# A per-token attention block on one core: block-diagonal stationary filled by DMA, token index innermost

## What is computed

```python
x = x + attn(layernorm(x))
x = x + ffn(layernorm(x))
# attn: q, k, v = h @ w.T + b, each (rows, 32 heads, 32)
#   scores = einsum('bshd,bstd->bsht', q, k) / sqrt(32); probs = softmax(scores)
#   context = einsum('bsht,bstd->bshd', probs, v)
# ffn: h @ base_w.T + base_b + 2 * (LoRA of the two best of 8 experts, rank 16, softmax weights)
```

## Time and profile before

| | before |
|---|---|
| median of 3 runs | 1545.02 us |
| profiled execution: span | 1543.5 us |
| TensorE busy | 1367.9 us (89%) |
| VectorE busy | 1261.1 us (82%) |
| ScalarE busy | 503.8 us (33%) |
| GpSimd busy | 210.7 us (14%) |
| 6144 small matmuls (L956 to L958) | 983.2 us busy, 176 ns each |
| 96 copies on ScalarE, 160 on VectorE (L308) | 182.1 us and 109.9 us |
| mean granted clock | 0.986 |

### The profile page before, as it was taken

How to read it: one execution, slowest core, us unless ns; L and a number is a source line. 1 busy time by engine, 2 the same in 40 slices (tenths; PEclk the granted TensorE clock), 3 DMA queues, 4 the chain that set the end, 5 groups by cost and what they waited for, 6 DMA issues and landing times.

```text
span 1543.5 us, 30006 instructions
## 1 busy us (share of the span) xinstructions
PE 1367.9 (89%) x12432; PEld 750.4 (49%) x12432; DVE 1261.1 (82%) x1751; ACT 503.8 (33%) x572; POOL 210.7 (14%) x280
## 2 busy tenths in 40 slices
PE   0777999999999999999999999999999999999996
PEld 0444445545544554554455455445545544554553
DVE  5778888888888888888888888888888888888874
ACT  7952222333222233322223332222333222233320
POOL 0011110011111001111100111110011111001110
PEclk9989999999999999999999999999999999999997
DMA  9401111000111100011110101111000111100000
GB/s 380 165 1 42 41 41 37 31 29 25 41 41 41 37 31 29 25 41 41 41 35 33 31 23 41 41 41 36 32 31 24 41 41 41 38 30 30 24 29 28
DMA packets 20208, 70.52 MB, mean 46 GB/s; under 512 B 2144, under 2 KB 3168, under 8 KB 20192
## 3 DMA queue, kind: packets, MB, share of 16 engines
q1 hardware_dynamic: 20192, 70.30, 12.8%
HBM read 53.51 MB, written 16.78 MB: 46 GB/s over the span
## 4 chain that ended last, share of the span: by engine, by line
DVE 61%; PE 14%; issue 10%; ACT 6%; DVEq 5%; DMA 3%; SPq 0%; POOL 0%; ACTq 0%; POOLq 0%
DVE work L308 6%; DVE work L800 6%; DVE x_lo L684 5%; PE acc L965 5%; DVE work L725 5%; PE acc L976 5%; DVE work L872 4%; DVE work L843 4%; DVE work L718 4%; DMA work<-x_dram 3%; DVE work L794 3%; DVE work L889 3%; DVE work L911 3%; DVEq L751 3%; DVE work L906 2%
## 5 line engine op out<-in xcount | busy, mean ns | idle before, releaser
L1018 PE MATMUL acc<-base_parts,x_hi 128*128 128x512 f16 x1024 | 325.0, 381 | 32.4 <-DVE work L308 32.4
L956 PE MATMUL attn_ps<-work 128*128 128x32 f16 x2048 | 329.0, 177 | 2.7 <-DVE work L718 1.7
L957 PE MATMUL attn_ps<-work 128*128 128x32 f16 x2048 | 327.3, 176 | 0.0
L958 PE MATMUL attn_ps<-work 128*128 128x32 f16 x2048 | 326.9, 176 | 0.0
L957 PEld LDWEIGHTS attn_ps<-work 128*128 128x128 f16 x2048 | 189.7, 96 | 201.6
L308 ACT COPY work<-work 32x2048 f16<-32x2048 f16 x96 | 182.1, 1897 | 139.2 <-DVE work L718 88.3
L956 PEld LDWEIGHTS attn_ps<-work 128*128 128x128 f16 x2048 | 193.7, 96 | 6.0 <-issue 3.6
L965 PE MATMUL acc<-w_hi_k,x_hi 128*128 128x512 f16 x512 | 140.6, 385 | 62.1 <-DVE work L718 28.4
L1018 PE MATMUL acc<-base_parts,x_lo 128*128 128x512 f16 x512 | 194.4, 380 | 0.0
L958 PEld LDWEIGHTS attn_ps<-work 128*128 128x128 f16 x2048 | 188.9, 96 | 0.0
L668 DVE BATCH_NORM_STATS2 stats<-work 128x6 f32<-128x512 f32 x128 | 82.3, 685 | 126.4 <-DMA work<-x_dram 125.3
(11 more groups left out here) (135 smaller groups left out, 2231.4 us busy)
## 6 DMA issues: line engine op xcount, KB each, us to landing
work<-x_dram SPq DMA_DIRECT2D x64, 512.0 KB, 3.5
out_dram<-work SPq DMA_DIRECT2D x32, 512.0 KB, 2.8
work<-wT_dram SPq DMA_DIRECT2D x19, 512.0 KB, 9.5
v_parts<-wT_dram SPq DMA_DIRECT2D x8, 512.0 KB, 14.8
base_parts<-wT_dram SPq DMA_DIRECT2D x5, 512.0 KB, 12.1
biases_sb<-bias_dram SPq DMA_DIRECT2D x4, 512.0 KB, 15.2
work<-agT_dram SPq DMA_DIRECT2D x1, 544.0 KB, 4.7
lora_up<-lora_b_dram SPq DMA_DIRECT2D x1, 512.0 KB, 15.8
```

The costliest lines, as they stand in the source:

```text
L956: nc.tensor.matmul(dst, diag[:, i, 0, :], moving[:, i, 0, :], start=True, stop=False)
L957: nc.tensor.matmul(dst, diag[:, i, 0, :], moving[:, i, 1, :], start=False, stop=False)
L958: return nc.tensor.matmul(dst, diag[:, i, 1, :], moving[:, i, 0, :], start=False, stop=True)
L1018: nc.tensor.matmul(dst, rows_part[:, m // 3, :], w_part[:, m // 3, cols], start=(m == 0), stop=False)
```

## The change

The layouts of `diag`, `k_parts` and `parts` are turned: part a outermost, the token index t innermost. The transposes of q, k and v then write `turned` densely, and TensorE reads its stationary operand, and the moving operand of the scores, with a step of 32 values (64 bytes). The probabilities keep their order within a part (`probs`, another view of the same buffer), so that their moving operand stays dense. The blocks of `diag` are filled by DMA: eight copies SBUF to SBUF for q and eight for v, each of 32 partitions x 1024 fp16 (64 KB), issued by SyncE, four when the high part is there and four when the low part is. `qdiag_ready` and `vdiag_ready` count their landings. VectorE's transpose of v no longer waits for the q block (only for q's low part). The copies on ScalarE and VectorE are gone.

```diff
-        diag = carve(block_diag_len).bitcast(F16).rearrange("p (t a c) -> p t a c", t=QD, a=2)
+        diag = carve(block_diag_len).bitcast(F16).rearrange("p (a m t) -> p a m t", a=2, t=QD)
...
-        k_parts = carve(HID).bitcast(F16).rearrange("p (t a c) -> p t a c", t=QD, a=2)
+        k_parts = carve(HID).bitcast(F16).rearrange("p (a c t) -> p a c t", a=2, t=QD)
...
-        parts = carve(HID).bitcast(F16).rearrange("p (t a c) -> p t a c", t=QD, a=2)
+        parts_all = carve(HID).bitcast(F16)
+        parts = parts_all.rearrange("p (a c t) -> p a c t", a=2, t=QD)
+        probs = parts_all.rearrange("p (a t c) -> p a t c", a=2, t=QD)
...
-        Q_ACT, Q_DVE = (0,), (1, 2, 3)
-        V_ACT, V_DVE = (0, 1), (2, 3)
-        turned3 = turned.rearrange("p (t c) -> p t c", t=QD)
-
-        def spread_quadrant(copy, g, ready):
-
-            s = slice(g * QD, (g + 1) * QD)
-            copy(diag[s, :, :, s], parts[s, :, :, :]).then_inc(ready, 1)
+        turned3 = turned.rearrange("p (u v) -> p u v", u=QD)
+        SPREAD = 16 * 2 * NQ
...
+            def spread(a, ready):
+
+                for g in range(NQ):
+                    s = slice(g * QD, (g + 1) * QD)
+                    sp.dma_start(diag[s, a, s, :], parts[s, a, :, :]).then_inc(ready, 16)
...
+                sp.wait_ge(q_hi_ready, t + 1)
+                spread(0, qdiag_ready)
+                sp.wait_ge(q_lo_ready, t + 1)
+                spread(1, qdiag_ready)
+
+                sp.wait_ge(v_hi_ready, t + 1)
+                sp.wait_ge(scored, t + 1)
+                spread(0, vdiag_ready)
+                sp.wait_ge(v_lo_ready, t + 1)
+                spread(1, vdiag_ready)
+                if prev:
                     store(t - 1)
...
-                act.wait_ge(q_lo_ready, t + 1)
-                for g in Q_ACT:
-                    spread_quadrant(nc.scalar.copy, g, qdiag_ready)
...
-                act.wait_ge(qdiag_ready, NQ * (t + 1))
+                act.wait_ge(qdiag_ready, SPREAD * (t + 1))
...
-                spread_quadrant(nc.scalar.copy, V_ACT[0], vdiag_ready)
...
-                spread_quadrant(nc.scalar.copy, V_ACT[1], vdiag_ready)
...
-                act.wait_ge(vdiag_ready, NQ * (t + 1))
-                nc.scalar.copy(parts[:, :, 0, :], turned3).then_inc(p_hi_ready, 1)
+                act.wait_ge(vdiag_ready, SPREAD * (t + 1))
+                nc.scalar.copy(probs[:, 0, :, :], turned3).then_inc(p_hi_ready, 1)
...
-                nc.vector.transpose(turned.rearrange("p (t h) -> p h t", t=QD), ev_heads).then_inc(qt_ready, 1)
+                nc.vector.transpose(turned, ev).then_inc(qt_ready, 1)
...
-                dve.wait_ge(q_lo_ready, t + 1)
-                for g in Q_DVE:
-                    spread_quadrant(nc.vector.tensor_copy, g, qdiag_ready)
...
-                dve.wait_ge(qdiag_ready, NQ * (t + 1))
-                nc.vector.transpose(turned.rearrange("p (t d) -> p d t", t=QD),
-                                    ev.rearrange("p (h d) -> p d h", h=HEADS)).then_inc(vt_ready, 1)
+                nc.vector.transpose(turned3, ev.rearrange("p (h d) -> p d h", h=HEADS)).then_inc(vt_ready, 1)
...
-                for g in V_DVE:
-                    spread_quadrant(nc.vector.tensor_copy, g, vdiag_ready)
...
-                nc.tensor.matmul(dst, diag[:, i, 0, :], moving[:, i, 0, :], start=True, stop=False)
-                nc.tensor.matmul(dst, diag[:, i, 0, :], moving[:, i, 1, :], start=False, stop=False)
-                return nc.tensor.matmul(dst, diag[:, i, 1, :], moving[:, i, 0, :], start=False, stop=True)
+                hi, lo = (probs[:, a, i, :] if moving is probs else k_parts[:, a, :, i] for a in range(2))
+                nc.tensor.matmul(dst, diag[:, 0, :, i], hi, start=True, stop=False)
+                nc.tensor.matmul(dst, diag[:, 0, :, i], lo, start=False, stop=False)
+                return nc.tensor.matmul(dst, diag[:, 1, :, i], hi, start=False, stop=True)
```

More of the change, by code:

```diff
@@ L353, in _ @@
             load("base")
-            sp.wait_ge(w_lo_done, n_split)
-            sp.dma_start(res, rows(x, 0)).then_inc(res_loaded, 16)
+            def spread(a, ready):
+                for g in range(NQ):
+                    s = slice(g * QD, (g + 1) * QD)
+                    sp.dma_start(diag[s, a, s, :], parts[s, a, :, :]).then_inc(ready, 16)
             def store(p):
@@ L371, in step @@
                     sp.dma_start(res, rows(x, t)).then_inc(res_loaded, 16)
+                else:
+                    sp.wait_ge(diag_zero, 1)
+                sp.wait_ge(q_hi_ready, t + 1)
[8 more added lines that the diff above has]
+                if prev:
                     store(t - 1)
+                else:
+                    sp.wait_ge(w_lo_done, n_split)
+                    sp.dma_start(res, rows(x, 0)).then_inc(res_loaded, 16)
             pipeline(sp, step, lambda t: store(t - 1))
@@ L406, in k_low_part @@
                 pool.wait_ge(k_hi_ready, t + 1)
-                nc.gpsimd.tensor_tensor(k_parts[:, :, 1, :], turned3, k_parts[:, :, 0, :],
+                nc.gpsimd.tensor_tensor(k_parts[:, 1, :, :], turned3, k_parts[:, 0, :, :],
                                         ALU.subtract).then_inc(k_lo_ready, 1)
@@ L525, in k_high_part @@
                 act.wait_ge(kt_ready, t + 1)
-                nc.scalar.copy(k_parts[:, :, 0, :], turned3).then_inc(k_hi_ready, 1)
+                nc.scalar.copy(k_parts[:, 0, :, :], turned3).then_inc(k_hi_ready, 1)
             k_high_part(0)
@@ L552, in step @@
                     act.wait_ge(ctx_acc, t)
-                nc.scalar.copy(parts[:, :, 0, :], turned3).then_inc(q_hi_ready, 1)
-                if not prev:
-                    act.wait_ge(diag_zero, 1)
-                act.wait_ge(q_lo_ready, t + 1)
-                for g in Q_ACT:
-                    spread_quadrant(nc.scalar.copy, g, qdiag_ready)
+                nc.scalar.copy(parts[:, 0, :, :], turned3).then_inc(q_hi_ready, 1)
                 if nxt:
@@ L713, in attention_scales, with low_part @@
                 assert a_steps[0] == A_STEPS
-            def low_part(t, hi_ready, lo_ready):
+            def low_part(t, split_of, hi_ready, lo_ready):
                 dve.wait_ge(hi_ready, t + 1)
-                nc.vector.tensor_tensor(parts[:, :, 1, :], turned3, parts[:, :, 0, :],
+                nc.vector.tensor_tensor(split_of[:, 1, :, :], turned3, split_of[:, 0, :, :],
                                         ALU.subtract).then_inc(lo_ready, 1)
@@ L820, in take_k @@
                     dve.wait_ge(p_lo_ready, t)
-                nc.vector.transpose(turned.rearrange("p (t h) -> p h t", t=QD), ev_heads).then_inc(kt_ready, 1)
+                nc.vector.transpose(turned, ev).then_inc(kt_ready, 1)
             def first_k():
@@ L852, in step @@
                         normalise(t + 1, 0, ld, rstd1, xn1_ready)
-                low_part(t, q_hi_ready, q_lo_ready)
-                if not prev:
-                    dve.wait_ge(diag_zero, 1)
-                dve.wait_ge(q_lo_ready, t + 1)
-                for g in Q_DVE:
-                    spread_quadrant(nc.vector.tensor_copy, g, qdiag_ready)
+                low_part(t, parts, q_hi_ready, q_lo_ready)
                 if not prev:
@@ L913, in step @@
                     finish(t - 1, 0)
-                low_part(t, p_hi_ready, p_lo_ready)
+                low_part(t, probs, p_hi_ready, p_lo_ready)
                 if prev:
@@ L1033, in context_ready @@
             def context_ready(p):
-                pe.wait_ge(vdiag_ready, NQ * (p + 1))
+                pe.wait_ge(vdiag_ready, SPREAD * (p + 1))
                 pe.wait_ge(p_lo_ready, p + 1)
@@ L1055, in step @@
                     context_ready(t - 1)
-                project(t, "k", 1, 1, k_acc, any_low[0], moving=parts if prev else None)
+                project(t, "k", 1, 1, k_acc, any_low[0], moving=probs if prev else None)
                 if prev:
@@ L1062, in step @@
                     pe.wait_ge(w_lo_done, (Q_ + 1) * KC)
-                project(t, "q", 0, 2, q_acc, any_low[0], moving=parts if prev else None, first=2 * KC,
+                project(t, "q", 0, 2, q_acc, any_low[0], moving=probs if prev else None, first=2 * KC,
                         attended=ctx_acc if prev else None)
@@ L1091, in step @@
                 pe.wait_ge(k_lo_ready, t + 1)
-                pe.wait_ge(qdiag_ready, NQ * (t + 1))
+                pe.wait_ge(qdiag_ready, SPREAD * (t + 1))
                 if prev:
@@ L1123, in tail @@
                 for i in range(QD):
-                    small = attend_one(parts, i)
+                    small = attend_one(probs, i)
                 small.then_inc(ctx_acc, 1)
```

7 lines of the change are left out of this document (2 added, 5 removed).

## The result

The changed kernel takes 1739.25 us (median of 4 runs, 1736.77 to 1739.87); the kernel before, on the same chip, 1545.34. The ratio is 1.1251, with a 95% interval of 1.1235 to 1.1267: 194 us slower, where 1521 was forecast and 1657 was the upper end. The profiled execution has a span of 1735.0 us.

What follows compares the result with a forecast made beforehand. VectorE was taken to bound each pass up to the context, TensorE from there. A gain of 0.78 us over 31 passes, 24 us off the median 1545.0, gave 1521; own range 1502 to 1540, 8 in 10 within 1502 to 1657.

Steps and rivals of the forecast that it cites:

- The three waits: In each pass: TensorE waits for a DMA before the scores, VectorE for the scores before the maximum and ScalarE before the sum.
- the turn to TensorE: Before the row maximum: VectorE gets there at 14.3 us and waits for TensorE's scores, done at 16.25.
- the exponential bared: In the softmax: ScalarE's exponential, 1.15 us, is no longer hidden by two VectorE copies of 1.41 us.
- the gain of 0.78 us a pass: At the context's start: TensorE free at 26.70 us into the pass, where the context began at 27.48 before.
- TensorE's price: Extra time of stepped reads on 136 bare stationary loads: taken as 0, bounds 0 and +79 ns a load.
- The second rival: Scores and context: steps slow TensorE by 1.6 to 2, 2.4 to 4.4 us a pass, 1596 to 1657 us; chance 0.27.
- S: Start of the scores on TensorE, counted from the query transpose: forecast 8.4 us (7.8 to 9.0), against 8.06 before.
- the fourth rival: Transposes: dense writes bring nothing; only the value's could stay at 2.1 us, with 1.9 us of slack; no chance given.
- Query spread: Before the scores: eight SyncE copies replace VectorE's three (2.12 us); an issue takes 0.33 us, landing 2.2 us.

Runs made afterwards that it cites:

- e1: The changed kernel, but TensorE reads both small operands densely from the same buffers (wrong places); 1528.71 us, ratio 0.989 to the kernel before.
- e3: The changed kernel with only the scores' moving operand read with a step, the stationary read densely (wrong places); 1639.46 us.
- e4: The kernel before, copies and transposes unchanged, with TensorE's stationary and the scores' moving operand read with a 64-byte step (wrong places); 1677.38 us.
- e11: e1 with four copies of 128 KB for q and four for v, in place of eight and eight; 1552.08 us.

## Why the prediction was wrong

**Bound and shape of the pass:** right. The three waits, the turn to TensorE and the exponential bared (VectorE waits 1.22 us for it) came as worked out. e1, which is the change without the steps' price, took 1528.7 us, within the 1502 to 1540 given for that case, but that is luck. Its context starts 27.57 us into the pass, the kernel before's at 27.49: the gain of 0.78 us a pass did not come. The pass is shorter by 0.6 us all the same, because the residual fell from 2.8 us to 2.2, which the sum did not have.

**TensorE's price, taken as 0: the step that failed.** I took 0 "because this is a read, and the row nearest to a stepped read shows none". That row was the context's transpose, 1250 ns. It reads PSUM. The value's transpose, which reads SBUF with a step of 128 bytes, stays at 1957 ns when its write is dense (e1): a stepped read of SBUF costs VectorE the same as a stepped write there, 1958. The trace before could not tell this, as the one transpose that reads SBUF with a step also wrote with one; but it did show that the free row read another memory. By e1 to e3 the stationary's step is worth 160 us, the moving operand's 111, both 210, of which some 30 are the lower clock that came with them.

**The second rival was the right one, and its size was short.** It had 40 to 53 ns in place of 25.5 on 160 places, 2.4 to 4.4 us a pass. Measured: 61 to 66 ns behind a bare load, 57 for a moving operand alone, some 70 with both. With 70 on the 96 small matmuls of the scores and 64 on the context's 64 bare ones, its own sum is 96 x 44.5 + 64 x 38.5 ns = 6.7 us a pass. e4 has 6.5: 4.0 in the scores (the maximum comes 3.1 later, and before VectorE reached it 1.0 us after the scores' end) and 2.4 from the sum to the context's transpose (18.67 for 16.23). The fault was to carry a factor from VectorE's rows to TensorE. The time per value would have come nearer for the moving operand: 57 ns for 32 columns are 1.8 ns each, and VectorE's stepped transposes took 1.96 us for 1024 values, 1.9 ns each, a number that was to be had from the earlier trace rows. For the stationary operand it would not, since 128 values load in 61 to 66 ns, 0.5 ns each; so this agreement is one pair of numbers and not shown to be a rule. The rival's top of 1657 was passed by 82 us, 2.6 a pass: 2.3 from this size, 0.9 from the later S, which the rival had left at 8.4, and 0.9 from the lower clock, less 1.5 from the shorter residual. The value's transpose of the fourth rival did stay at 1.95, in its slack, as said there.

**Query spread, a term that was mis-sized too:** landing was 2.0 us for 2.2. The issue was mis-sized: 0.51 to 0.59 us for 0.33, taken from a load of 128 rows, and the low part's four stood behind the high part's, which I had called hidden. S is 9.3 in place of 8.4. These 0.9 us are more than the whole gain of 0.78 that was forecast: in e1 they eat it, and its 17 us come from the residual (0.6 us by 31 passes).

**Missed altogether:** the residual. It fell from 2.8 to 1.28 us because the longer context moved it away from GpSimd's work (in e4, whose copies and transposes are those of before, it is 1.28), and so hid 1.5 us a pass of the loss.

## What to carry to other kernels

Before TensorE or VectorE is made to walk SBUF with a step, count how many values share 16 bytes: here four fp16 values in 16 bytes cost TensorE nothing and two cost it 8 to 12 ns a load, and runs of two fp32 values cost VectorE's transposes nothing. A value with 16 bytes to itself took 1.8 ns in a moving operand (step of 64 bytes), 1.9 ns in a transpose (128 bytes) and 0.5 ns in a stationary load (16, 32 and 64 bytes alike), which is 2.5 times the dense load. A layout with a short run on one side and a short step on the other (pairs of tokens) gave both engines their dense price. And a row vouches for another only if it reads the same memory: here the row from PSUM said nothing of SBUF. Last, when a variant comes out at the forecast time, look whether it got there by the forecast way: e1 did not.

## What the runs showed of the hardware that I had not expected

- A step in the stationary operand does not slow a load to the 104 ns of an fp32 one: 61 to 66 ns at steps of 16, 32 and 64 bytes alike.
- A transpose on VectorE reads PSUM with a step of 128 bytes at the dense price (1250 ns), SBUF not (1957).
- An issue on SyncE takes 0.33 us for a load of 128 rows and 0.51 to 0.60 for a copy within SBUF of 32 rows, of 64 KB or of 128 KB.
- VectorE's residual, with two operands in SBUF, takes 1.28 us, and made next to no headway beside GpSimd's low part, which also reads two: in four traces where they overlap it ends 1.08 us after that does.
- The granted clock can fall behind one wait and not behind the next of the same length: behind 2.5 us it fell in 9 of 20 passes of e11, and each fall cost 1.3 us of the scores.
